# Token attention: transposed scores eight steps behind the maxima products, value pairs in odd steps

## What is computed

```python
# x: (8, 750, 128); q, k, v: 8 heads of 16, 748 rows each
q = proj(x, WQ, BQ)          # elu(conv1d(x, W, 3 taps) + b), likewise k and v
scores = einsum('bhqd,bhkd->bhqk', q, k) / sqrt(16)
attn = softmax(scores, axis=-1)
out = einsum('bhqk,bhkd->bhqd', attn, v)
...
h = h + gated_attention(layernorm(h))
h = h + mixture_of_experts(layernorm(h))
```

## Time and profile before

| | |
|---|---|
| median of 3 runs | 838.88 us (836.3 to 841.2) |
| the profiled execution | 836.78 us, span 834.8 us |
| busy in the span | PE 95%, PEld 58%, DVE 81%, ACT 62%, POOL 31% |
| mean granted TensorE clock | 0.984 |
| token stage | from the start to about 536 us |
| turns of the maxima (L698) | 32 |

### The profile page before, as it was taken

One profiled execution on the slowest core, in us unless ns is written; L12 is line 12 of the kernel. 1 busy time (PEld: TensorE's weight loads), 2 busy tenths in 40 slices (PEclk: granted clock), 3 DMA queues, 4 the chain that ended last, 5 costly groups with the idle time before them and its releaser, 6 DMA issues. The chain is left out here.

```text
span 834.8 us, 15533 instructions
## 1 busy us (share of the span) xinstructions
PE 794.7 (95%) x5651; PEld 484.6 (58%) x5651; DVE 673.1 (81%) x1619; ACT 519.8 (62%) x1127; POOL 259.4 (31%) x253
## 2 busy tenths in 40 slices
PE   9799999999999999999999999879999999999996
PEld 5354554554554554454554444457778778787775
DVE  4898889889889889889889887577777887777854
ACT  4177776776776776776777777553564645646432
POOL 3562331331331341340341303222224333242222
PEclk9799999999999999999999999989999999999999
DMA  5360050050050051061041001000000000000001
GB/s 120 63 118 16 6 117 14 2 114 20 3 107 27 2 106 29 2 102 33 1 82 35 1 1 52 0 1 1 1 20 1 20 19 1 20 1 20 20 1 37
DMA packets 32427, 27.92 MB, mean 33 GB/s; under 512 B 5248, under 2 KB 31072, under 8 KB 32352
## 3 DMA queue, kind: packets, MB, share of 16 engines
q1 hardware_dynamic: 32112, 26.64, 15.5%
q10 hardware_dynamic: 240, 0.30, 0.2%
HBM read 4.76 MB, written 3.06 MB: 9 GB/s over the span
## 5 line engine op out<-in xcount | busy, mean ns | idle before, releaser
L429 ACT ACTIVATE probs<-ps_a 128x384 f32<-128x384 f32 (+1 forms) x732 | 299.7, 487 | 76.1 <-PE ps_a L625 71.1
L521 DVE TENSOR_REDUCE neg_max<-ps_a 128x1 f32<-128x512 f32 (+1 forms) x384 | 256.3, 683 | 55.3 <-PE ps_a L641 54.0
L625 PE MATMUL ps_a<-q_rep,k_rep 98*128 98x384 bf16 (+3 forms) x768 | 228.1, 323 | 1.3 <-DVE neg_max L523 1.2
L641 PE MATMUL ps_a<-k_rep,q_rep 96*128 96x512 bf16 (+3 forms) x768 | 218.5, 327 | 6.8 <-DVE neg_max L521 3.5
L656 PE MATMUL ps_pv<-probs,v_hat 128*32 128x364 f32 (+3 forms) x1536 | 140.6, 483 | 0.0
L641 PEld LDWEIGHTS ps_a<-k_rep,q_rep 96*128 96x128 bf16 (+1 forms) x768 | 76.3, 103 | 109.4 <-DVE neg_max L521 36.0
L523 DVE TENSOR_REDUCE neg_max<-ps_a 128x2 f32<-128x472 f32 x192 | 123.0, 641 | 0.0
L625 PEld LDWEIGHTS ps_a<-q_rep,k_rep 98*128 98x128 bf16 (+1 forms) x768 | 79.0, 104 | 58.1 <-ACT probs L429 30.3
L656 PEld LDWEIGHTS ps_pv<-probs,v_hat 128*32 128x32 f32 (+1 forms) x1536 | 40.1, 109 | 64.3 <-issue 58.5
L972 POOL TENSOR_SCALAR rs_v<-mv 128x6 f32<-128x6 f32 x8 | 2.0, 254 | 185.1 <-DVE mv L958 185.1
L258 POOL TENSOR_SCALAR qk_e<-qk_e 128x748 f32<-128x748 f32 x14 | 38.0, 2716 | 29.8 <-ACT qk_e L333 29.8
(11 more groups left out here) (222 smaller groups left out, 1225.6 us busy)
## 6 DMA issues: line engine op xcount, KB each, us to landing
q_rep<-parts_q SPq DMA_DIRECT2D x96, 96.0 KB, 3.7
k_rep<-parts_k SPq DMA_DIRECT2D x93, 96.0 KB, 3.6
xT<-in_x SPq DMA_DIRECT2D x8, 375.0 KB, 4.2
out_h<-y_out SPq DMA_DIRECT2D x7, 320.0 KB
q_rep<-max_T SPq DMA_DIRECT2D x32, 6.0 KB
w_sb<-in_w_T SPq DMA_DIRECT2D x2, 256.0 KB, 3.0
out_h<-y_out SPq DMA_DIRECT2D x8, 54.0 KB
k_rep<-parts_k ACTq DMA_DIRECT2D x3, 96.0 KB, 4.2
```

The source lines that it names most:

```text
L429: act.activation(probs[0:rows(kt), n % RING, 0:w], ps_a[0:rows(kt), 3 + n % 3, 0:w], ACT.Exp, scale=DH ** -0.5).then_inc(p_ready, 1)
L521: dve.tensor_reduce(neg_max[0:rows(t), 0, col:col + 1], ps_a[0:rows(t), c, :], AX.X, ALU.max, negate=True).then_inc(sc_max, 1)
L625: pe.matmul(out[0:rows(kt), 0:QW[qh]], k_rep[0:KM, cb % 2, h, kt * P:kt * P + rows(kt)], q_rep[0:KM, cb % 2, qh, h, 0:QW[qh]], start=True, ...
L641: last = pe.matmul(out, q_rep[0:KS, it % 2, t // QT, h, t % QT * P:t % QT * P + rows(t)], k_rep[0:KS, it % 2, h, 512:L] if c == 2 else k_r ...
```

## The change

`LAG` goes from 9 to 8. With it the value pairs, which follow the transposed scores, move to odd steps: the step with the pair (`pair_step`) is now odd and the one without (`single_step`) even. `turn` moves into `single_step`, behind the second transposed scores. The banks of the transposed scores are counted from `FIRST_PAIR`. In the tail the last two output transposes come a step earlier (`turns`).

```diff
-LAG = 9
+LAG = 8
...
+    FIRST_PAIR = GH * (STEPS - LAG)
+
+    def st_bank(n):
+        return 3 + (n - FIRST_PAIR) % 3
+
     def pair_slot(n):
-        return ps_a[:, n // 2 % 3 * 2:n // 2 % 3 * 2 + 2, :]
+        k = (n - FIRST_PAIR) // 2 % 3 * 2
+        return ps_a[:, k:k + 2, :]
...
-            out = ps_a[:, 3 + n % 3, :]
+            out = ps_a[:, st_bank(n), :]
...
-        def even_step(it, s, c):
+        def pair_step(it, s, c):
             if c:
                 scores_T(it, *c, 0)
             scores(it, s, 0)
             if c:
                 scores_T(it, *c, 1)
             apply_pair(it, s)
-            turn(it, s)
             scores(it, s, 1)
...
-        def odd_step(it, s, c):
+        def single_step(it, s, c):
             if c:
                 scores_T(it, *c, 0)
             scores(it, s, 0)
             if c:
                 scores_T(it, *c, 1)
+            turn(it, s)
             scores(it, s, 1)
...
-                (even_step, odd_step)[s % 2](it, s, probs_step(it, s))
+                (single_step, pair_step)[s % 2](it, s, probs_step(it, s))
```

More of the change, by code:

```diff
@@ L428, in _ @@
                         else:
-                            act.activation(probs[0:rows(kt), n % RING, 0:w], ps_a[0:rows(kt), 3 + n % 3, 0:w], ACT.Exp,
+                            act.activation(probs[0:rows(kt), n % RING, 0:w], ps_a[0:rows(kt), st_bank(n), 0:w], ACT.Exp,
                                            scale=DH ** -0.5).then_inc(p_ready, 1)
@@ L608, in scores_T @@
             n, h = GH * cs + j, GH * g + j
-            out = ps_a[:, 3 + n % 3, :]
+            out = ps_a[:, st_bank(n), :]
             if it == B:
                 out = pair_slot(n)[:, j % 2, :]
-                if j % 2 == 0 and n < GH * (STEPS - LAG) + 4:
+                if j % 2 == 0 and n < FIRST_PAIR + 4:
                     pe.wait_ge(sc_max, it * 72)
-                if j % 2 == 0 and n > GH * (STEPS - LAG):
+                if j % 2 == 0 and n > FIRST_PAIR:
                     pe.wait_ge(p_ready, cb * 96 + n - 4)
@@ L618, in scores_T @@
             else:
-                pe.wait_ge(z_copied, (4, 5, CONVS + 2)[n])
+                pe.wait_ge(z_copied, (4, 5, CONVS + 2)[st_bank(n) - 3])
             if cb < 2 and n == 0:
```

## The result

| | us |
|---|---|
| before | 839.0 |
| after | 876.2 |
| ratio after / before | 1.046 (95% interval 1.0436 to 1.0485) |
| forecast | 860, range 843 to 869, slower 0.80 |

The change makes the kernel 37 us slower. The direction was as forecast; the loss is 1.7 times the forecast 21.5 us and the time lies above the range. The medians are of four executions each, and one of the four after took 2808 us and is left out of the ratio; nothing here says why. The profiled execution took 876.19 us, its span is 874.3 us, against 836.78 and 834.8 before.

The account below looks back on a forecast made before the run. PE's in-order list was taken as the bound. Uncovered turn waits net of what comes back, 19.6 us in passes 1 to 7 and 1.4 in the first, plus ramps 0.5, made 21.5 us: 860, range 843 to 869.

Parts of the forecast that it names:

- What bounds the kernel: Mid-stage token steps: PE's in-order list sets the time; PE waits are paid in full, DVE's free while PE has work.
- rival (A): PE isn't the limit, VectorE at 88% is (skill's busy-share rule); the wait is absorbed: 836 to 843, chance 0.12.
- The cost of (2), steps 0, 6 and 18: PE waits at the turn, no longer covered by a pair: 0.82, 0.82 and 1.28 us (0.97 more than today).
- The upper bound, the distances in today's rows: Waits at the four turns without help of a pair step ahead: 5.1 us in a pass.
- The cost of (2), step 12: PE waits 0.61 us for max_parts at the turn of step 12, with a shorter copy hold-up and six-product chunk.
- The clock: PE's granted clock stays at 1.00 despite waits of 0.8 us: nothing; a fall priced only inside rival (C).
- rival (C): Rows of maxima come late as well, landings as in the worst row: 21 us more, 870 to 885; chance 0.10.
- What comes back: Short PE waits in steps 12 to 17 go: 0.4 us credited, net 2.8 us a pass.
- the ramps: Both ends change by a step: 1.5 us more in the scored steps, 1 us less in the tail; +0.5.
- the rows of maxima: Transfer into q_rep, two steps instead of three between turn and transposed scores: taken as in time, 0.
- the microsecond credited there: Tail up to the next stage's first product, 23.8 us, a step less: -1 us.

Follow-up runs that it names:

- turns early (best): Kernel before, with the second head group's output transposes in steps 15 and 16 instead of 16 and 17; 833.7 us, ratio 0.996.
- eight steps, even pairs: Changed kernel (LAG 8), but value pairs in even steps, turn behind the pair, ring 20 instead of 16, smaller warm-up operands; 837.4 us, ratio 1.000.
- both together: LAG 8 with value pairs and turn in even steps, ring 20, plus output transposes in steps 15 and 16; 836.6 us, ratio 0.998.
- maxima already there: On top of middle part late: PE turns the previous quarter's max_parts from a second buffer; 845.4 us, ratio 1.008.
- turn behind the third scores: On top of middle part late: turn moved behind its step's third scores, last transposed scores between it and the chunk; 855.0 us, ratio 1.020.
- middle part late: Changed kernel, with ACT's middle part of k after step 12 instead of 11, so POOL's L274 starts after the maxima; 861.6 us, ratio 1.027.
- turn ahead of the pair: Kernel before with one line moved: turn of the maxima ahead of its step's value pair, LAG 9 and even pairs kept; 877.1 us, ratio 1.045.

## Why the forecast missed its size

PE's idle time ahead of the turns by the view, the profiled execution, and a pass in mid-stage with no fall of the clock in it, from first scores to first scores, all in us:

```
kernel                         idle ahead of turns   profiled execution    pass
before                                 3.6                836.8            63.22
turns early (best)                     1.4                835.1            62.86
eight steps, even pairs                3.6                837.0            63.19
both together                          1.5                836.8            62.82
maxima already there                  10.2                848.5            64.52
turn behind the third scores           7.9                855.2            65.43
middle part late                      26.3                860.5            66.14
after                                 35.1                876.2            67.48
turn ahead of the pair                36.3                877.3            67.93
```

The idle time of the view is not a price list. It counts from modelled ends and so shows too little. Nor is the whole execution, since the first pass varies with the clock: that of the kernel with the turns early is 2.5 us longer than that of before, with the clock low already from 23.1 us. The pass is the better measure. By the spacing of PE's starts the four turns of such a pass wait 0.36 us before, 3.83 with the middle part late, 5.16 after and 5.17 with the turn ahead of the pair; the pass is longer than before by 2.9, 4.3 and 4.7 us. So a wait at the turn is paid nearly in full, and the two kernels with pairs in odd steps get some 0.5 us of it back. With the turn behind the third scores a part of the waits has moved to the chunk and to step 13, and the column of the turns doesn't show it.

**What bounds the kernel** was right. PE's list sets the time of the stage; both the rule as rival (A) read it and that rival are refuted by the one-line experiment: DVE, busy for 88% of a pass, waited for scores 13.1 us in a pass instead of some 6.8, and the time rose by 4.5%.

**The cost of (2), steps 0, 6 and 18** was right. Forecast were waits of 0.82, 0.82 and 1.28 us; by the spacing of PE's starts they are 0.90, 0.92 and 1.30. The view itself shows 0.76 for step 6 of a pass, since it counts from a modelled end. Rows of after for step 6 and for step 18:

```profile
175.32 0.32 PE L631 MATMUL ps_a<-q_rep,k_rep 98*128 98x364 bf16 x1
176.39 0.22 PE L704 MATMUL ps_misc<-ident_bf,max_parts 128*128 128x128 bf16 x1 [0.76 <-DVE max_parts L519]
176.45 0.38 PE L647 MATMUL ps_a<-k_rep,q_rep 96*128 96x512 bf16 x1
...
209.87 0.23 PE L704 MATMUL ps_misc<-ident_bf,max_parts 128*128 128x128 bf16 x1 [1.14 <-DVE hall L505]
```

The upper bound, the distances in today's rows, is what the one-line experiment cost: there steps 0, 6, 12 and 18 waited 1.44, 1.14, 0.78 and 1.83, and a pass grew by 4.7 us, where the bound said 5.1.

**The cost of (2), step 12** is the step that failed. The sum took 0.17 us for the last maxima operation in every quarter. In this quarter, in the trace of before, POOL's third part of k (L268 there, L274 after) started behind it by a margin of half a microsecond, first two rows; the last two show that an operation of this path had been held once even then:

```profile
304.61 0.17 DVE L513 TENSOR_TENSOR max_parts<-neg_both,max_parts 128x12 bf16<-128x12 f32 x1
...
305.09 1.61 POOL L268 TENSOR_TENSOR parts_k<-qk_e,parts_k 128x748 bf16<-128x748 f32 x1 [1.14 <-ACT parts_k L352]
...
66.01 2.09 POOL L891 TENSOR_SCALAR bias_fac<-bias_fac 128x748 f32<-128x748 f32 x1
...
66.20 0.64 DVE L509 TENSOR_TENSOR neg_both<-neg_max 128x12 f32<-128x12 f32 x1
```

The change turned step 11 into a pair step, and ACT's cast, which releases POOL, moved against DVE's copy: it starts 0.27 us ahead of the copy (192.11 and 192.38) instead of 0.29 behind it (304.16 and 303.87). That is the missing margin; why the cast comes earlier is not shown. Forecast 0.61 us, measured 2.06 by the spacing of starts; with the middle part late 0.72. For the seven passes 7 x 1.34 = 9.4 us, which is also most of DVE's 13 us of additional busy time. I had looked for what DVE waits for, and hadn't asked what else runs on POOL at that moment. At 66.20 L509 took 0.64 instead of 0.16 us while POOL's L891 ran: a sign was there, if a faint one, for L511 and L513 ran in 0.17 us each beside the rest of the same L891.

**The clock** was the second term put at nothing: it was priced only inside rival (C), with a reason taken from a wait of 0.31 us. It fell once in passes 1, 3 and 5, always behind the 2.06 us wait of step 12, and each such pass is 1.58 us longer than its neighbours (69.06 against 67.48 us): 4.7 us. The same wait in passes 2, 4 and 6 was followed by no fall. For waits of 0.9 to 1.3 us the assumption held, as the kernel with the middle part late shows. In the first pass the clock was low three times, from 23.9, 34.2 and 58.1 us, for 17 us in all, before only once, for 10 us. The last of the three lies behind the 2.06 us wait of step 12; the first lies ahead of the first turn, and the kernels with the turn ahead of the pair and with the turns early have such a fall as well, so it isn't the change's doing. That pass is 6.8 us longer, where 2.9 were forecast with the ramps and 1.3 belong to POOL. The Trainium skill (TensorE: Matmul & The Clock Gate, HAM oscillation — how this bites in real kernels) has the clock go down when TensorE idles between bursts of matmuls; the trace agrees in kind, with PE busy for 4.11 of the 6 us before the fall.

**What comes back, the ramps, the rows of maxima.** An undisturbed pass is 67.48 us instead of 63.22, of which 2.06 - 0.61 = 1.45 are step 12's excess: 2.81 for the rest, where 2.8 was forecast. Passes 6 and 7, which are shorter in both kernels, gave more back: pass 6 lost 3.5 us, 1.3 of them POOL's, and pass 7 lost 1.9 over its first 23 steps, where 2.8 each were forecast. Its last step, now a pair step, is 1.1 us longer, which belongs to the ramp. The tail from its first transposed scores to the next stage's first product is 23.8 us, the same as in the earlier trace rows; the microsecond credited there was not there. The rows of maxima were in time everywhere.

The sum with the measured terms: 21.5 + 9.4 (POOL) + 4.7 (clock in passes 1, 3, 5) = 35.6. Measured were 37.2 by medians and 39.4 between the profiled executions, and of the latter 0.8 us lie ahead of the first scores and some 2.6 in the first pass, where the clock was low for longer, in part by chance. The terms of POOL and of the clock were taken away at once by the kernel with the middle part late, which landed at 861.6, near the forecast. The traces part them: an undisturbed pass of that kernel is 1.34 us shorter than one of after, which is POOL's share, and a pass with a fall is another 1.58 longer.

## What to carry to other kernels

When steps of different weight alternate, an instruction that waits for another engine is paid by what stands ahead of it in its own queue: before moving heavy work to other steps, list every waiting instruction that it covered. Work that out from both sides, as here, and it is good to 0.1 us a place. And check for each small operation on that path what POOL does at the new time: a path of three operations of less than 0.2 us grew by 1.3 us here without a single semaphore.

## What the runs showed of the hardware

- DVE operations of 12 columns were held until the end of a wide POOL operation: a subtraction with two SBUF operands took 1.51 instead of 0.17 us beside POOL's tensor operation on 748 columns of 1.60 us, a cast 0.83 instead of 0.17 us beside a memset of 768 columns of 0.74 us. DVE's reductions from PSUM ran beside POOL's next operation in 0.7 us as ever. The Trainium skill (SBUF — State Buffer, Who interferes with whom) describes such a lock: a pair of SBUF ports shared by VectorE and GpSimd and held for the whole instruction by whoever issues first. The subtraction agrees with it; the cast agrees in its end, but by the profile it had started 0.07 us ahead of the memset. It was open to be used in the forecast and wasn't.
- Not every overlap holds DVE. In step 0 of the kernel before POOL's L980, a tensor operation with two SBUF operands of 6 columns that lasts 1.36 us, ran over all three maxima operations, and they took 0.16 and 0.17 us; by the lock as described the first and the last of them should have waited. The measurement decides: how long POOL's row is doesn't say for how long it holds.

```profile
334.99 1.36 POOL L980 TENSOR_TENSOR rs_all<-rs_v,half_neg 128x6 f32<-128x6 f32 x1
...
335.55 0.16 DVE L509 TENSOR_TENSOR neg_both<-neg_max 128x12 f32<-128x12 f32 x1
335.75 0.17 DVE L511 CAST max_parts<-neg_both 128x12 bf16<-128x12 f32 x1
335.96 0.17 DVE L513 TENSOR_TENSOR max_parts<-neg_both,max_parts 128x12 bf16<-128x12 f32 x1
```

- Beside L274 it was decided by tenths of a microsecond: a start 0.11 us behind POOL's cost 1.34 us, a start half a microsecond ahead of it cost nothing.
- TensorE's clock fell to 1.2 GHz in a stage where PE was busy for over 90%: in four of seven passes behind a wait of 2.06 us, and in the one-line experiment once at a turn that waited 1.8 us and once behind one that waited 1.4. The same waits in other passes were followed by none. With waits of at most 1.3 us, in the kernel with the middle part late, it stayed at 2.4 GHz in all passes behind the first.
